# P V products taken for two key blocks at a time, eight matmuls in one group instead of four

## The reference, cut to what matters

```python
xq, xk, xv = (x @ w.T for w in (wq, wk, wv))            # (4, 1024, 16, 32) each
scores = einsum('bqhd,bkhd->bhqk', xq, xk)              # no scaling
probs  = softmax(scores)
out    = einsum('bhqk,bkhd->bqhd', probs, xv) @ wo.T
x = layernorm(x + out)
logits = x @ Wr.T + br; e = argmax(softmax(logits)); weight = max(softmax(logits))
h = einsum('nd,erd->ner', x, A); y = einsum('ner,eor->neo', h, B) / 64
x = layernorm(x + y[n, e] * weight)
```

## Time and profile before

| | before |
|---|---|
| median of three executions | 1656.07 us |
| the profiled execution: time, span | 1657.02 us, 1655.2 us |
| TensorE, matmuls | 1574.9 us busy, 95% |
| GpSimd | 1175.8 us busy, 71% |
| VectorE | 941.8 us busy, 57% |
| ScalarE | 769.8 us busy, 47% |
| P V products (L572) | 2048 matmul passes, 2048 weight loads |
| mean granted TensorE clock | 0.991 |

### The profile page before, as it was taken

How to read it: one execution, slowest core, us unless ns; L and a number is a source line. 1 busy time by engine, 2 the same in 40 slices (tenths; PEclk the granted TensorE clock), 3 DMA queues, 4 the chain that set the end, 5 groups by cost and what they waited for, 6 DMA issues and landing times.

```text
span 1655.2 us, 19384 instructions
## 1 busy us (share of the span) xinstructions
PE 1574.9 (95%) x6432; PEld 756.3 (46%) x6432; DVE 941.8 (57%) x1688; ACT 769.8 (47%) x1409; POOL 1175.8 (71%) x653
## 2 busy tenths in 40 slices
PE   5989999999999999999999999999999999999797
PEld 2544444444444444444444444444444444444343
DVE  1646566655565567655456556665546677672433
ACT  1135555554455444445444444444544555555222
POOL 1058989988777677667778766677777888989500
PEclk9999999999999999999999999999999999999899
DMA  7443534332032332134332132322423122210001
GB/s 242 101 134 110 158 105 113 99 99 74 16 97 71 77 84 69 48 109 118 94 97 46 33 102 71 84 66 77 134 46 96 40 47 57 63 35 27 1 6 46
DMA packets 82067, 132.09 MB, mean 80 GB/s; under 512 B 18592, under 2 KB 36016, under 8 KB 81968
## 3 DMA queue, kind: packets, MB, share of 16 engines
q1 hardware_dynamic: 78704, 125.59, 27.5%
q0 software_dynamic: 1152, 4.22, 0.7%
q10 hardware_dynamic: 2112, 1.05, 0.2%
HBM read 87.84 MB, written 42.20 MB: 79 GB/s over the span
## 4 chain that ended last, share of the span: by engine, by line
PE 85%; DVE 6%; issue 3%; POOL 2%; DMA 2%; ACT 2%; SPq 1%; ACTq 0%; POOLq 0%; DVEq 0%
PE sc L560 15%; PE w L459 14%; PE pv L572 14%; PE mx L550 13%; PE w L470 7%; PE w L522 6%; PE w L481 5%; PE w L509 5%; DVE mxc L741 2%; PE w L503 1%; POOL Psum L393 1%; DVE eq L822 1%; DMA wqk_s<-wkT 1%; PE w L516 1%; PE w L531 1%
## 5 line engine op out<-in xcount | busy, mean ns | idle before, releaser
L741 DVE TENSOR_REDUCE mxc<-mx 128x1 f32<-128x512 f32 x1024 | 684.7, 686 | 553.8 <-PE mx L550 550.6
L393 POOL TENSOR_TENSOR Psum<-Psum,P 128x1024 f32<-128x1024 f32 x384 | 902.0, 2368 | 118.0 <-ACT P L630 113.5
L630 ACT ACTIVATE P<-sc 128x512 f32<-128x512 f32 x1024 | 594.1, 596 | 620.3 <-PE sc L560 612.1
L560 PE MATMUL sc<-stack 98*128 98x512 f32 x1024 | 679.8, 665 | 14.6 <-DMA stack<-mrow 12.5
L550 PE MATMUL mx<-stack 96*128 96x512 f32 x1024 | 413.1, 407 | 7.9 <-DVE mxc L741 7.9
L560 PEld LDWEIGHTS sc<-stack 98*128 98x128 f32 x1024 | 193.5, 189 | 292.6 <-issue 138.4
L389 POOL TENSOR_TENSOR Psum<-P 128x1024 f32<-128x1024 f32 x64 | 151.3, 2370 | 228.1 <-ACT P L630 221.0
L459 PE MATMUL w<-xT_s,wqk_s 128*128 128x512 f32 x512 | 265.3, 610 | 20.4 <-DMA wqk_s<-wkT 18.1
L550 PEld LDWEIGHTS mx<-stack 96*128 96x128 f32 x1024 | 195.7, 191 | 173.4 <-issue 137.3
L572 PE MATMUL pv<-P,V 128*32 128x512 f32 x2048 | 272.7, 605 | 0.0
L459 PEld LDWEIGHTS w<-xT_s,wqk_s 128*128 128x128 f32 x512 | 92.5, 191 | 103.1 <-issue 86.2
(11 more groups left out here) (108 smaller groups left out, 823.7 us busy)
## 6 DMA issues: line engine op xcount, KB each, us to landing
stack<-qk_parts SPq DMA_DIRECT2D x192, 256.0 KB, 5.4
qk_parts<-split SPq DMA_DIRECT2D x64, 512.0 KB, 2.8
xT_s<-xT SPq DMA_DIRECT2D x8, 1024.0 KB, 10.2
den_s<-den_parts SPq DMA_DIRECT2D x124, 64.0 KB, 2.0
r<-x SPq DMA_DIRECT2D x3, 2048.0 KB, 8.6
out<-r SPq DMA_DIRECT2D x12, 512.0 KB, 3.0
wqk_s<-wqT SPq DMA_DIRECT2D x14, 256.0 KB, 4.1
wqk_s<-wkT SPq DMA_DIRECT2D x14, 256.0 KB, 4.4
```

The costliest lines, as they stand in the source:

```text
L393: pool.tensor_tensor(Psum[:, s % 2, i, :], Psum[:, s % 2, i, :], P[:, unit % NP, :], ALU.add).then_inc(add_done, 1)
L560: pe.matmul(sc[c][:, :], stack(s, i)[0:KS, 0, 128 * kb:128 * kb + 128], stack(s, i)[0:KS, 1, 512 * c:512 * c + 512], start=True, stop=True ...
L630: act.activation(P[:, unit % NP, 512 * c:512 * c + 512], sc[c][:, :], ACT.Exp).then_inc(exp_done, 1)
L741: dve.tensor_reduce(mxc[:, q % 2, m:m + 1], mx[TURN[g] % NMX][:, :], AX.X, ALU.max).then_inc(mx_done, 1)
```

## The change

Two key blocks are taken in one group. `out_block(s, kb)` becomes `out_group(s, g)` with `g` from 0 to 3. A group issues the four matmuls of `kb = 2 g` and then the four of `kb = 2 g + 1`, with one wait ahead of the first and one rise of `pv_done` on the last. Groups 0, 1 and 2 stand at units 5, 9 and 13 (halves 11, 19 and 27) and group 3 at unit 1 of the next slot (half 3). The waits for `pv_done` on ScalarE are divided accordingly. The number of matmuls, the six places of `P`, the two sets of sums and the plan of chunks are as before.

```diff
+    GROUPS = KB // 2
...
-            def out_block(s, kb):
-                pe.wait_ge(exp_done, 2 * (UNITS * s + 2 * kb + 2))
+            def out_group(s, g):
+
+                pe.wait_ge(exp_done, 2 * (UNITS * s + 4 * g + 4))
                 if s % PAIRS == 0:
-                    pe.wait_ge(v_done, KB * (s // PAIRS) + kb + 1)
-                if kb == 0 and s:
+                    pe.wait_ge(v_done, KB * (s // PAIRS) + 2 * g + 2)
+                if g == 0 and s:
                     pe.wait_ge(pv_copied, s)
-                for c in range(2):
-                    for i in range(2):
-                        at, head = HD * (2 * c + i), 2 * (s % PAIRS) + i
-                        done = pe.matmul(pv[at:at + HD, :], V[:, kb, HD * head:HD * head + HD],
-                                         P[:, (UNITS * s + 2 * kb + i) % NP, 512 * c:512 * c + 512],
-                                         start=(kb == 0), stop=(kb == KB - 1))
+                for kb in (2 * g, 2 * g + 1):
+                    for c in range(2):
+                        for i in range(2):
+                            at, head = HD * (2 * c + i), 2 * (s % PAIRS) + i
+                            done = pe.matmul(pv[at:at + HD, :], V[:, kb, HD * head:HD * head + HD],
+                                             P[:, (UNITS * s + 2 * kb + i) % NP, 512 * c:512 * c + 512],
+                                             start=(kb == 0), stop=(kb == KB - 1))
                 done.then_inc(pv_done, 1)
...
                 if c == 1 and k == 1 and s:
-                    out_block(s - 1, KB - 1)
-                if c == 1 and k % 2 == 1 and k >= 3:
-                    out_block(s, (k - 3) // 2)
+                    out_group(s - 1, GROUPS - 1)
+                if c == 1 and k % 4 == 1 and k >= 5:
+                    out_group(s, (k - 5) // 4)
...
-            out_block(LAST, KB - 1)
+            out_group(LAST, GROUPS - 1)
...
                 if c == 0 and unit >= NP:
-                    act.wait_ge(pv_done, (unit - NP) // 2 + 1)
+                    act.wait_ge(pv_done, (unit - NP) // 4 + 1)
...
                 if n >= KB:
-                    act.wait_ge(pv_done, KB * (PAIRS * (n // KB) - 1) + n % KB + 1)
+                    act.wait_ge(pv_done, GROUPS * (PAIRS * (n // KB) - 1) + n % KB // 2 + 1)
...
-                act.wait_ge(pv_done, KB * (s + 1))
+                act.wait_ge(pv_done, GROUPS * (s + 1))
```

## The result

The changed kernel took 1652.8 us (median of 20 executions, 1645.9 to 1659.8) against 1655.9 us for the kernel before (median of 20); the ratio is 0.9975, 95% interval 0.9964 to 0.9986. It is faster, but by 3 us (0.25%) where I had predicted 25, and it lies outside my range of 1617 to 1643 us. The profiled execution took 1651.8 us, with a span of 1650.0.

What follows compares the result with a forecast made beforehand. TensorE was taken as the bound, GpSimd second in places. 128 groups saving 0.27 us each gave 35 us, less 9.8 given back: 25 us off the profiled 1657.0, 1632; predicted 1631 us, 8-in-10 range 1617 to 1643.

Steps and rivals of the forecast that it cites:

- The nine plain slots: Slots 7 to 9, 15 to 17 and 23 to 25, without expert work: each should be 1.1 us shorter.
- Rivals 1 and 3: First: array runs empty between key blocks, 1642 us, 12%; third: weight loads exposed in rounds three and four, 1741 us, 5%.
- The rule of the Trainium skill on row groups: In P V groups: weight loads overlap running matmuls only in different row groups, so none of the second block's is hidden.
- The waits. None is added: Step claiming groups add no wait on exponentials, `P` or copies; ScalarE edits and halved signals cost nothing.
- What moves, and what is given back: Cover lost where blocks go or groups lengthen: four terms, together 9.8 us given back, between 1 and 22.
- `t2`: Five pieces behind a removed block, slots 10, 11, 18, 19 and 28, lose cover: 4 us together, 0 at least.
- GpSimd: Last six groups save nothing, half the gain of slots 27 to 29 goes: 3.2 us, at most 13.
- rival 2: GpSimd becomes the bound in all light slots, giving back 13 us instead of 3.2: 1641 us, chance 13%.
- The loop of score and exponential: With two `sc` banks, longer runs of bare halves wait for exponentials: 1.5 us, between 0 and 4.
- The maxima's row: First score after slots with few chunks waits for `stack<-mrow`, four times, 0.27 us longer each: 1.1 us.

Runs made afterwards that it cites:

- three pairs of runs: Kernel before and changed kernel, each with gate instructions left out (1645.7, 1616.6 us), gate in one instruction (1643.0, 1617.3), or GpSimd's additions in two pieces (1651.5, 1629.1).

## Why the prediction was wrong

**What held.** TensorE was the bound, at 1.19 us a block. The group in four rounds, no load of weights in the open, no new wait of the group itself: all as forecast, with 2.05 us for 2.11. The second block cost 0.86 us, the two full-width passes that I had given as its lower bound. The nine plain slots which I had said would each be 1.1 us shorter were 1.5 us shorter, and so were the two others. Rivals 1 and 3 did not come about.

The rule of the Trainium skill on row groups ("TensorE: Matmul & The Clock Gate", Part 3, The mechanism), which I had weighed, would have made the change a loss. The trace does not agree with it: the loads at 852.77 and 853.20 ran under matmuls of the same row groups.

**What failed** is the step "The waits. None is added", and with it the sum of "What moves, and what is given back". I had let VectorE off as idle half the time, with three `mx` banks to hold 2 us of its work, and given it no term but `t2`. The runs show that there were new waits: TensorE waits 16.5 us more at `mx` and `hm`, because GpSimd's additions hold `gate` and `eq` on VectorE for up to 2.4 us at a time and everything behind them stands too. I summed 9.8 us, at most 22; measured, 42 us of gain less the 3 to 5 that came leaves some 38. Term by term:
- *The term that was not there: VectorE held by GpSimd.* I had used VectorE's mean share, "ScalarE and VectorE idle half the time", and costed its side at nothing. The rows that spoke against it stood in the profile before (busy us, mean ns):

```profile
L827 DVE TENSOR_SCALAR gate<-eq,eqm,lrec 128x8 f32<-128x8 f32 x32 | 35.9, 1123 | 1.2
L822 DVE SCALAR_TENSOR_TENSOR eq<-lsb,lmax,rank 128x8 f32<-128x8 f32 x32 | 31.8, 993 | 0.0
```

  Their shortest took 0.29 and 0.21 us. A mean of 1 us said that they were held, and how long, and what stood behind them, depends on phase, which the change shifts. With the holds mended in one way or another the change is worth 29, 26 or 22 us (three pairs of runs) instead of 3: 19 to 26 us of the missing 38. The low clock behind the long waits is part of that figure; I can't split it off exactly.
- *`t2`.* I had said that a `t2` loses its cover where a block goes. In slot 11, where it waited 0.39 us before, it now waits 1.38:

```profile
578.02 0.40 PE L551 MATMUL mx<-stack 96*128 96x512 f32 x1
579.80 0.66 PE L517 MATMUL w<-ident,hm 128*128 128x128 f32 x4 [1.38 <-DVE r L806]
```

  All waits of `t2` for VectorE grew by 2.9 us; I had said 4. They are the same 11.7 us with one gate instruction, so they are lost cover and not holds.
- *GpSimd.* Slots 27 to 31, where I gave back 3.2 us in all, are 3.4 us longer than before the change. Without gate instructions slots 26 to 31 gain the same 3.9 us before and after, so the six slots gave back all of their 8 us, as rival 2 has it, but at the end only. ScalarE's waits for an addition grew from 7.1 to 13.4 us, which fits; no run shows by itself that GpSimd is the cause there. The last wait for GpSimd answers to the earlier trace rows, 2.98 us for 2.05:

```profile
1547.07 1.06 PE L532 MATMUL w<-Psum,ones 128*32 128x512 f32 x8 [2.98 <-POOL Psum L394]
```
- *The loop of score and exponential* was priced as 1.5 us; TensorE's waits for an exponential grew from 1.1 to 3.0 us.
- *The maxima's row* was priced as 1.1 us; the waits are 12.2 us in total for 12.5, but two of them stand at the start of a stretch of low clock. Slots 2, 5 and 6 together got 1.2 us longer instead of 4 us shorter, each with 3.4 us at the low clock.

**The clock** I had not put among the rivals. It cost at most 14 us, half of that at the held `hm`: with one gate instruction the mean was 0.991 again. But the three low stretches in slots 2, 5 and 6 stay in the run without gate instructions (at 179, 281 and 319 us), where they follow waits for a DMA, so it isn't holds alone. What exactly brings them about was not tried and stays open.

**Range and chances.** I gave 93% to a gain over 0.2% and got one of 0.25%. That this came out right is luck: moving the group by one unit changed the time by as much as the whole gain. The upper end of the range took rivals 1 and 2 one at a time. The range failed since every way in my list of give-backs was a small, local one, and I had no term for what a shift in phase does to engines that meet by accident.

## What to carry to other kernels

Before you predict a change that moves work in time, look for instructions whose mean is far above their minimum (here 1123 against 290 ns): something holds them, and the change draws their lot anew. Price cover by what stands behind it in the buffer ring, not only by the engine's queue: `den` one half later cost 32 us by uncovering one bank, and the group one half earlier gained 17 us, more than the some 9 us that sharing the way in and out can give (31 times 0.3, an estimate). Put work of the same narrow shape together, since each way in and out of it cost some 0.3 us here.

## What was not expected of the hardware

- A VectorE instruction on 128x8 numbers took up to 2.44 us beside GpSimd additions of 128x1024 in the changed kernel, up to 5.20 us (one `eq`) in the kernel before, and at most 1.39 us beside additions of 128x512; alone 0.21 to 0.29 us. Its end fell within 0.06 us of the end of a GpSimd instruction each time that it took over 0.4 us in the changed kernel. The additions took 2.34 to 2.40 us throughout, so they did not wait in turn.
- The way in and out of narrow matmuls is paid once for adjacent work even when bank and weights differ: P V and `den`, six rounds in 2.72 us.
- What brings the clock to 1.2 GHz can't be read from the length of the wait ahead of it. In the changed kernel the granted clock was 0.50 for 3 to 7 us at or after waits of TensorE of 2.38 us (three times) and 2.01 us, but also at 1.18 and 1.24 us, and once, at 1473.4 us, with no wait over 0.3 us ahead. It stayed at 1.00 after a fourth wait of 2.38 us (at 515.24), after one of 2.60 us (at 1088.64), and after the 2.67 us in the kernel before.
